# W1 in eight weight pieces and the LayerNorm sum on VectorE: a macaron layer on eight cores

## What is computed

```python
x = x + 0.5 * _L0_ffn_ref(_layernorm(x), U, V, W1, b1, W2, b2)
x = x + _L0_attn_ref(_layernorm(x), Wq, Wk, Wv, Wo)
x = x + 0.5 * _L0_ffn_ref(_layernorm(x), U, V, W1, b1, W2, b2)

def _L0_ffn_ref(x, U, V, W1, b1, W2, b2):
    h = relu(einsum('bsd,de->bse', x, W1) + b1)
    alpha = softmax(einsum('bse,ek->bsk', h, W2) + b2)
    vx = einsum('krd,bsd->bskr', V, x)
    uvx = einsum('kdr,bskr->bskd', U, vx)
    return einsum('bsk,bskd->bsd', alpha, uvx)
```

## Time and profile before

| | |
|---|---|
| median of the runs | 3488.93 us |
| lowest and highest of three runs | 3378.17 and 3524.61 us |
| the profiled execution | 3382.42 us |
| its span, slowest core (core 0) | 3380.9 us |
| spans of the eight cores | 3350.1 to 3380.9 us |
| busy: PE, PEld, DVE, ACT, POOL | 2334.1, 1123.2, 917.9, 733.2, 60.3 us |
| DMA, mean share of the 16 engines | 157.52 MB written, 47 GB/s |

### The profile page before, as it was taken

How to read it: one execution, slowest core, us unless ns; L and a number is a source line. 1 busy time by engine, 2 the same in 40 slices (tenths; PEclk the granted TensorE clock), 3 DMA queues, 4 the chain that set the end, 5 groups by cost and what they waited for, 6 DMA issues and landing times. The chain is left out here.

```text
span 3380.9 us, 34762 instructions; the slowest of 8 cores (3350.1 to 3380.9 us)
## 1 busy us (share of the span) xinstructions
PE 2334.1 (69%) x12146; PEld 1123.2 (33%) x12236; DVE 917.9 (27%) x1922; ACT 733.2 (22%) x1346; POOL 60.3 (2%) x61
## 2 busy tenths in 40 slices
PE   3594658768677597557735956587686775975657
PEld 2252324333333243323222523243343332432222
DVE  3102431412503314501331024314125033154004
ACT  4120131311202113411041201413112021135110
POOL 0000000000000000000000000000000000000000
PEclk9797879889789798778867978798897897986778
DMA  5313213033051230133263131120320513201432
GB/s 151 50 26 50 28 22 50 1 50 50 1 75 26 40 61 1 26 50 52 85 187 50 26 50 25 26 50 1 50 50 1 75 26 50 50 1 26 62 63 100
DMA packets 103130, 157.52 MB, mean 47 GB/s; under 512 B 2076, under 2 KB 92208, under 8 KB 98352
## 3 DMA queue, kind: packets, MB, share of 16 engines
q0 software_dynamic: 97296, 117.48, 23.2%
q1 hardware_dynamic: 5664, 37.81, 3.0%
HBM read 255.98 MB, written 16.78 MB: 81 GB/s over the span
## 5 line engine op out<-in xcount | busy, mean ns | idle before, releaser
L507 PE MATMUL pg<-XnT,wSA 128*128 128x512 bf16 (+1 forms) x1536 | 316.2, 373 | 128.7 <-DMA wSA<-wk 122.0
L353 PE MATMUL pg<-XnT,wSB 128*128 128x512 bf16 (+1 forms) x1280 | 265.3, 365 | 122.6 <-DMA wSB<-w 122.6
L686 PE MATMUL pg<-wSB,aoAll 128*128 128x512 bf16 x992 | 263.5, 411 | 56.0 <-DVE Xb L693 38.8
L522 PE MATMUL pg<-wSA,XnT 128*128 128x512 bf16 x1240 | 296.0, 394 | 2.6 <-issue 0.7
L353 PE MATMUL pg<-XnT,wSA 128*128 128x512 bf16 (+1 forms) x1280 | 281.1, 381 | 12.0 <-DVE XnT L270 12.0
L507 PEld LDWEIGHTS pg<-XnT,wSA 128*128 128x128 bf16 x1536 | 159.9, 105 | 282.7 <-issue 173.4
L597 ACT ACTIVATE Praw<-pS,att 128x384 f32<-128x384 f32 x256 | 148.8, 581 | 389.0 <-DVE att L587 372.4
L366 ACT ACTIVATE h_s<-pg,b1T 128x512 bf16<-128x512 f32 (+1 forms) x160 | 103.1, 645 | 571.0 <-PE pg L353 569.7
L536 PE MATMUL pg<-XnT,wSB 128*128 128x512 bf16 x1024 | 222.3, 379 | 0.0
L693 DVE TENSOR_TENSOR Xb<-Xb,pg 128x512 f32<-128x512 f32 x256 | 175.9, 687 | 116.3 <-PE pg L686 111.3
L571 PE MATMUL pS<-Mk,Mq 4*128 4x384 bf16 x256 | 97.2, 380 | 153.5 <-ACT Praw L597 153.5
(11 more groups left out here) (71 smaller groups left out, 1957.6 us busy)
## 6 DMA issues: line engine op xcount, KB each, us to landing
Xb<-x SPq DMA_DIRECT2D x20, 1024.0 KB, 27.2
wSA<-w POOLq DMA_DIRECT2D x8, 2048.0 KB, 18.6
wSB<-w POOLq DMA_DIRECT2D x8, 2048.0 KB, 22.3
wSA<-wk POOLq DMA_DIRECT2D x8, 2048.0 KB, 18.6
wSB<-wq POOLq DMA_DIRECT2D x8, 2048.0 KB, 28.5
wSA<-wv POOLq DMA_DIRECT2D x8, 2048.0 KB, 14.9
wSB<-wo POOLq DMA_DIRECT2D x8, 2048.0 KB, 13.9
y<-Xb SPq DMA_DIRECT2D x16, 1024.0 KB, 4.1
```

The source lines that it names most:

```text
L353: t0=t0, nt=nt: e.matmul(bank[:, 0:nt * 128], slot[:, cc * 512 + s4 * 128: cc * 512 + (s4 + 1) * 128], xnt_rhs(t0, nt, cc), start=(cc == 0 ...
L507: e.matmul(bank[:, 0:nt * 128], wS[0][:, cc * 512 + h * 128: cc * 512 + (h + 1) * 128], xnt_rhs(i0, nt, cc), start=(cc == 0), stop=(cc == ...
L522: p.op("tensor", lambda e, bank=bank, l=l, cc=cc: e.matmul(bank[:, :], XnTS(l, cc), wS[0][:, cc * 512:(cc + 1) * 512], start=(cc == 0), st ...
L686: e.matmul(wbank[:, :], aoAll[:, slot * 512 + h2 * 128: slot * 512 + (h2 + 1) * 128], wS[1][:, h2 * D + cg * 512: h2 * D + (cg + 1) * 512] ...
```

## The change

There are four edits.

1. **Sum on VectorE.** The sum over a tile moves from ScalarE to VectorE: a `tensor_scalar` that multiplies by 1 and adds 0 with an accumulated output, into a scratch area of its own. ScalarE keeps the sum of squares.
2. **Eight weight pieces of 256 columns** in place of four of 512, in the same two buffers. A load writes 1 MB. A piece of g has two column groups in place of four.
3. **Logits per piece.** Each call has two matmuls in place of four, and there are eight rounds over the tiles in place of four. Since a g now has fewer pieces of work (six for ten tiles, four for eight) than tiles, the calls left over follow behind the last piece, one after another.
4. **LayerNorm emission in g = 0.** Before a piece whose tiles aren't all ready, `ln` is called for the tiles in the queue first, and the drain comes only when the queue is empty.

```diff
         def stage1(l):
             if wait_dx:
                 p.wait("scalar", dxv[(c, l)][0], dxv[(c, l)][1])
-            p.op("scalar", lambda e, l=l: e.activation(
-                sink, XS(l), AF.Copy, accum_out=sl(0, l)), inc=s_st)
-            p.wait("scalar", s_st)
+                p.wait("vector", dxv[(c, l)][0], dxv[(c, l)][1])
+            p.op("vector", lambda e, l=l: e.tensor_scalar(
+                sink2, XS(l), 1.0, 0.0, ALU.mult, ALU.add, accum_out=sl(0, l)))
...
         def emit_logits(g, i, l):
...
-            for s4 in range(4):
+            for s4 in range(2):
...
-        for g in range(4):
+        for g in range(8):
             slot = wS[g % 2]
             if g < 2:
-                dma_w(("w1", c, g), "AB"[g % 2], slot_dst(slot, 16, 512),
-                      wpiece_cols(dw1, g * 512))
+                dma_w(("w1", c, g), "AB"[g % 2], slot_dst(slot, 16, 256),
+                      wpiece_cols(dw1, g * 256, 256))
             wait_w("tensor", ("w1", c, g))
             if g == 0:
-                pieces = [(s4, t0, nt) for (t0, nt) in tsubs for s4 in range(4)]
+                pieces = [(s4, t0, nt) for (t0, nt) in tsubs for s4 in range(2)]
...
                     if g == 0:
-                        if any(l2 not in ln.te for l2 in range(t0, t0 + nt)):
-                            ln.drain()
+                        while any(l2 not in ln.te for l2 in range(t0, t0 + nt)):
+                            if lnq:
+                                ln(lnq.pop(0))
+                            else:
+                                ln.drain()
...
                 hev_bank[pi % 2] = s_hev.n
+            if g > 0:
+                for i2 in range(len(pieces), n):
+                    emit_logits(g - 1, i2, tiles[i2])
             hev_end[g] = s_hev.n
-            if g + 2 < 4:
+            if g + 2 < 8:
                 p.wait("gpsimd", s_hmm)
...
-            emit_logits(3, i, l)
+            emit_logits(7, i, l)
...
-            ln1 = make_ln(c, [pT0, pT1], h_s[:, 5120:5120 + 2048], wait_dx=True)
+            ln1 = make_ln(c, [pT0, pT1], h_s[:, 5120:5120 + 2048],
+                          h_s[:, 7168:7168 + 2048], wait_dx=True)
```

More of the change, by code:

```diff
@@ L217, in ph_loadx, with make_ln @@
             dxv[(c, l)] = (sem, sem.n)
-    def make_ln(c, pT, sink, wait_dx=False):
+    def make_ln(c, pT, sink, sink2, wait_dx=False):
         s_st, s_ma, s_rs, s_ap = S("st"), S("ma"), S("rs"), S("ap")
@@ L315, in emit_logits @@
                     hsl(g, s4, i * 128, (i + 1) * 128),
-                    W2b[:, (g * 4 + s4) * 8:(g * 4 + s4 + 1) * 8],
-                    start=(s4 == 0), stop=(s4 == 3)),
-                    inc=(s_lgm if s4 == 3 else None))
+                    W2b[:, (g * 2 + s4) * 8:(g * 2 + s4 + 1) * 8],
+                    start=(s4 == 0), stop=(s4 == 1)),
+                    inc=(s_lgm if s4 == 1 else None))
             p.wait("vector", s_lgm)
@@ L327, in ph_ffn_w1 @@
         lnq = list(tiles[4:]) if ln is not None else []
-        for g in range(4):
+        for g in range(8):
             slot = wS[g % 2]
             if g < 2:
-                dma_w(("w1", c, g), "AB"[g % 2], slot_dst(slot, 16, 512),
-                      wpiece_cols(dw1, g * 512))
+                dma_w(("w1", c, g), "AB"[g % 2], slot_dst(slot, 16, 256),
+                      wpiece_cols(dw1, g * 256, 256))
             wait_w("tensor", ("w1", c, g))
             if g == 0:
-                pieces = [(s4, t0, nt) for (t0, nt) in tsubs for s4 in range(4)]
+                pieces = [(s4, t0, nt) for (t0, nt) in tsubs for s4 in range(2)]
             else:
-                pieces = [(s4, t0, nt) for s4 in range(4) for (t0, nt) in tsubs]
+                pieces = [(s4, t0, nt) for s4 in range(2) for (t0, nt) in tsubs]
             for pi, (s4, t0, nt) in enumerate(pieces):
@@ L354, in ph_ffn_w1 @@
                              bank[:, 0:nt * 128],
-                             slot[:, cc * 512 + s4 * 128: cc * 512 + (s4 + 1) * 128],
+                             slot[:, cc * 256 + s4 * 128: cc * 256 + (s4 + 1) * 128],
                              xnt_rhs(t0, nt, cc),
@@ L367, in ph_ffn_w1 @@
                                   bank[:, 0:nt * 128], AF.Relu,
-                                  bias=b1T[:, g * 4 + s4: g * 4 + s4 + 1]),
+                                  bias=b1T[:, g * 2 + s4: g * 2 + s4 + 1]),
                      inc=s_hev)
                 hev_bank[pi % 2] = s_hev.n
+            if g > 0:
+                for i2 in range(len(pieces), n):
+                    emit_logits(g - 1, i2, tiles[i2])
             hev_end[g] = s_hev.n
-            if g + 2 < 4:
+            if g + 2 < 8:
                 p.wait("gpsimd", s_hmm)
-                dma_w(("w1", c, g + 2), "AB"[g % 2], slot_dst(wS[(g + 2) % 2], 16, 512),
-                      wpiece_cols(dw1, (g + 2) * 512))
+                dma_w(("w1", c, g + 2), "AB"[g % 2], slot_dst(wS[(g + 2) % 2], 16, 256),
+                      wpiece_cols(dw1, (g + 2) * 256, 256))
         for i, l in enumerate(tiles):
-            emit_logits(3, i, l)
+            emit_logits(7, i, l)
     uxv = {}
@@ L810, in build_nc @@
             A = (Kb, Vt, Qb, Praw, Pn, PTs, aoAll, att4, pS, pPT)
-            ln2 = make_ln(c, [pPT], Qb[:, 0:2048], wait_dx=False)
+            ln2 = make_ln(c, [pPT], Qb[:, 0:2048], Qb[:, 2048:4096], wait_dx=False)
             for hg in range(cfg.get("hgs", 4)):
@@ L826, in build_nc @@
             pT1 = fs.enter_context(nc.psum_tensor(un("pT1"), [128, 1024], BF16))
-            ln3 = make_ln(c, [pT0, pT1], h_s[:, 5120:5120 + 2048], wait_dx=False)
+            ln3 = make_ln(c, [pT0, pT1], h_s[:, 5120:5120 + 2048],
+                          h_s[:, 7168:7168 + 2048], wait_dx=False)
             ph_ffn_w1(c, list(range(1, 9)), h_s, plg, ln=ln3)
```

## The result

The changed kernel takes 3476 us (median of 8 runs) against 3379 us for the kernel before (median of 10). The ratio is 1.029, with a 95% interval from 1.027 to 1.032: slower by about 99 us. In the profiled executions it is 3468.6 against 3382.4. The three runs shown before the prediction had a median of 3489; with more runs the profiled 3382 turns out to be near the usual time of the kernel before. In some executions the cores of one die show a lower granted clock and the time is up to 9% longer; the ratios leave these out, and for the last two experiments, which have no ratio, single other times are given.

The account below looks back on a forecast made before the run. Each FFN stage was taken as bound by LayerNorm in its first W1 piece, then a queued wSB load, then TensorE. FFN1 +25.2, FFN3 +44.2 and attention +7.2 made +76.6 on 3382.4: 3459 us, range 3415 to 3580.

Parts of the forecast that it names:

- I take -13 us for each of four stages: Idle time before the wSB matmuls: halved loads shorten it by 13 us a stage, bounds -15 to 0.
- the rival in which it goes: Rival on the wSB gap: the change removes it, 4 x 17.6 us less, 3389 us; chance 0.03.
- The turn of 8.8 us: First LayerNorm: square roots of the first four tiles stand 8.8 us apart in place of 6.4.
- -2.5, for both chunks: FFN1 up to W1: half a load lands the few us earlier that the new chain needs, -2.5; if not, 0.
- 3 x 2.4 - 2.1: FFN1 up to W1: VectorE's sums less ScalarE's relief on the first tile make the chain 5.1 us late.
- Calls of 0.67 us: Four leftover logits calls behind each piece g = 1 to 7: 0.67 us each, 2.7 a piece, 18.9 a stage.
- 17.6 + 2.7 = 20.3 us each: FFN1 after the gap: seven half pieces with leftover calls and 2 us slow start, 144.1 us, or +35.1.
- The rival on TensorE's clock: Rival: TensorE's clock falls at each piece's end, during the leftover calls; +56, 3515 us; chance 0.12.
- The rival with the double rate: Rival: VectorE's sum takes 1.5 us in place of 2.4, 31 us less, 3428 us, +1.4%; chance 0.20.
- If each costs the slow start of 2.0 us, 28 of them are +56: Size of the clock rival: a 2.0 us slow start behind each piece's leftover calls, 3515 us; chance 0.12.
- a first row of a piece above 5 us: Sign named for a wrong forecast, in TensorE's first W1 matmuls of a piece.
- Packets: Rival: packets set the loads, so with 4128 as before the gap stays at 30.7; +52, 3511 us; chance 0.10.

Follow-up runs that it names:

- the last two experiments: Changed kernel with VectorE's sum of the next tile ahead of the copies: 3454 us; changed kernel with logits in four rounds, each over two pieces: 3392 and 3408 us.
- the early load: Changed kernel with the load of piece 1 issued at the stage's start, right behind that of piece 0: ratio 1.0072, 3404 us.
- the last experiment: Changed kernel, eight weight pieces, logits again in four rounds of four matmuls, each spread over two pieces: 3392 and 3408 us.
- the sum at another place: Changed kernel with VectorE's sum of the next tile queued ahead of the two copies of the tile before: 3454 us in one execution.
- two banks: Changed kernel with the logits' PSUM results in two banks in turn, a call waiting for the addition before the last: ratio 1.0123, 3421 us.

## Why the prediction was right or wrong

The forecast was 3459 us, +76.6 on the profiled execution or +2.3%; the ratio is +2.9% (2.7 to 3.2). The direction was right, the main mechanisms were too, and the time is in the range; the size was 20 us short. Three terms of the sum were mis-sized, which make the difference between 76.6 and the table's 97.5 with 1 us for attention.

- **The gap: 8 of the 20 us.** "I take -13 us for each of four stages" took its length from core 0, with 122.6 us in all. By the medians the gaps were 109.4 us in the table (111.6 as idle time) and shrank by 43.7, not 52. On the two slowest cores 122.6 fell to 68.3, or -13.6 a stage, as forecast; but core 0 had the longest gap of the eight in each of the four stages before, while core 5 after, with 68.3 us, is like its median (68.1). A wait read on one core was taken for all. That the gap would stay at all was read rightly from the order; the rival in which it goes needed the early load, which then gave 69 us.
- **g = 0 and the LayerNorm: 7.5 us.** The turn of 8.8 us held, and so did the square roots in g = 0 (tile 5 at 12.0 us behind W1's start where 11.75 was added up, tile 7 at 29.7 for 29.1). The step that failed most is "-2.5, for both chunks", up to W1 in FFN1: the medians are -1.4 and -0.3. The chain itself was right. From the landing of x to the first tiny operations it is 3.5 us in place of 5.6 on all eight cores, the 2.1 us that "3 x 2.4 - 2.1" counts. But now the LayerNorm sets W1's start, on every core, and with it the landing of x, which in the first chunk came 1.4 us later by the medians; why is open. In the second chunk W1 had started 2.4 us sooner than in the first already before, so there was less to gain. Then on core 5 g = 0 itself took 58.5 us where 56.8 were added up: the second tile group began 0.8 us late, its first row behind an idle TensorE took 6.4 us where I had put 5.6, and the two narrow pieces 6.4 for 6.
- **Pieces: 4 us.** Calls of 0.67 us were forecast and 0.68 measured. But "17.6 + 2.7 = 20.3 us each" halved a piece of 35.6 us to 17.6, and one of 28.4 to 14.0; without leftover calls a piece measured 17.8 and 14.2 (the last experiment). Pieces took 20.5 and 16.9 us, 5.6 us more over all 28. The rival on TensorE's clock adds 2.6 a core (below). Together that is more than the 4; what came back is not assigned.
- **The base** was chosen well: 3382 us is near the usual time of the kernel before. By the median of the three runs first shown, 3489, the same ratio would have been 3591 us, above the range.
- **The sum's duration** was taken at 2.3 us and is 2.29, with 0.08 to read it. It was chosen by the rows of reducing operations against the rule of the Trainium skill (VectorE: DVE Perf Modes, The perf-mode tier table) that `tensor_scalar` on fp32 runs at twice the rate. The trace names the instruction TENSOR_SCALAR_CACHE_REDUCE: with an accumulated output it isn't timed like the plain one of that row, which L255 bears out with 1346 ns. The rival with the double rate, given 0.20, fell with this.
- **Clock.** "If each costs the slow start of 2.0 us, 28 of them are +56" was far too much, and none at all would be wrong as well: "a first row of a piece above 5 us", named as a sign of being wrong, does occur. On the eight cores leftover calls are followed by the first row of the next piece 192 times; 14 of these rows took over 0.5 us more than the usual 3.61, 5.0 to 5.3 us, and none of the 672 other wide rows behind a stage's first. They cost 2.6 us a core. Two other traces with the same leftover calls have 27 such rows of 192 (early load) and 16 of 192 (the sum at another place). One of them on core 5, at 237.16, with its stretch (granted clock 0.68) and that of the usual row at 155.14 (1.00):

```profile
236.93 0.19 PE L313 MATMUL plg<-W2b,h_s 128*128 128x8 bf16 x2 [0.48 <-DVE lgacc L320]
237.16 5.30 PE L356 MATMUL pg<-XnT,wSA 128*128 128x512 bf16 x16
...
237.16:242.46 5.30, 5.30 (x19) 2.13 (x20) 0.16 (x1) 0.00 (x0) 0.00 (x0) 0.68 0.94 110
...
155.14:158.70 3.56, 3.56 (x19) 1.67 (x20) 0.16 (x1) 0.00 (x0) 0.00 (x0) 1.00 0.94 102
```

  The DMA engines are equally busy in both. With two banks, or with no leftover calls, there is no such row. So the 2.7 us of mostly idle TensorE brought them about, but seldom; why at one place and not at another is open. The Trainium skill (TensorE: Matmul & The Clock Gate, Part 1: The HAM clock gate) lets the clock follow recent activity; the granted clocks above agree, but by that alone one could not say how often a short pause is enough.
- **Packets** didn't set the gap: as many of them at half the size took 11 us less by the medians.

By the experiments' stretches the loss reads like this. The sum on VectorE costs 63 us (sum back on ScalarE), and the leftover calls cost 74 (logits in four rounds), of which two banks give back half (28 times 1.35 us; the rest of their 54 comes from the last calls and the slow rows). The smaller gap gives 44 back. Behind the gap the kernel without leftover calls is still 62 us longer than the kernel before: the half piece of W1 in each stage that used to be in g = 0. Against that, with the sum back on ScalarE the stretches to the end of g = 0 are 58 us shorter than before (20.4, 10.1, 17.7 and 9.6); 18 of these are the emission order's, alone on the kernel before, and the rest is less W1 work and the first weights, which were not taken apart. 63 + 74 - 44 + 62 - 58 is 97 us. So the half piece was nearly paid for by the shorter way to the end of g = 0; the sum and the leftover calls, 137 us, had only the smaller gap against them.

## What to carry to other kernels

Moving work to the less busy engine pays only if that engine isn't the one on the chain: read the turn of the loop (here VectorE ended it, at 6.4 us), not the busy time (22.0 us of VectorE against 28.2 of ScalarE in the first W1 piece). When a loop is cut finer, count what no longer fits between its parts; ten calls that hid between twelve pieces of work found only six. And before making a late load smaller, look at what stands ahead of it in its queue: issuing it early was worth 119 us in the kernel before, making it half as big 44.

## What the runs showed of the hardware

- A `tensor_scalar` with an accumulated output takes 2.29 us for 2048 fp32 elements, against 1.35 without one. This was expected of the rows, but that an added result makes it 1.7 times as long is worth knowing. On ScalarE the same sum (L231 before) takes 1.91 us and 0.19 to read it.
- The loads of 1 MB, with twice as many packets to a byte, have a median landing of 9.9 and 10.0 us on the page, against 18.6 and 22.3 us for those of 2 MB before. Both medians mix loads that run alone with pairs.
- The waits for the same load differ between cores that run the same program: 30.7 us a stage on core 0 before against 27.9 for the median core.
- TensorE's granted clock at times falls behind 2.7 us of short matmuls with waits between: at 14 of 192 such places here, 16 and 27 of 192 in two other traces. The next 16 wide matmuls then take 5.0 to 5.3 us in place of 3.6.
